# Causal attention in a chained kernel: k's rotation goes ahead a step, and the stage's first steps are put in another order

## What is computed

```python
resid = hidden_states
h = _rmsnorm(hidden_states, ln1_w)
q = (h @ Wq).reshape(B, S, NH, HD)      # NH = 32, HD = 128
k = (h @ Wk).reshape(B, S, KVH, HD)     # KVH = 4
v = (h @ Wv).reshape(B, S, KVH, HD)
q = _rope(q, pos); k = _rope(k, pos)
k = jnp.repeat(k, 8, axis=2); v = jnp.repeat(v, 8, axis=2)
scores = jnp.einsum('bqhd,bkhd->bhqk', q, k) / jnp.sqrt(jnp.float32(HD))
attn = jax.nn.softmax(jnp.where(causal, scores, -1e9), axis=-1)
o = jnp.einsum('bhqk,bkhd->bqhd', attn, v).reshape(B, S, NH * HD) @ Wo
x = resid + o
```

## Time and profile before

| | |
|---|---|
| median of 3 runs | 1162.79 us (1161.12 to 1169.5) |
| profiled execution | 1166.56 us, span 1164.8 us |
| mean granted TensorE clock | 0.955 |
| PE | 1042.5 us busy, 89% of the span |
| PE's weight loads | 914.2 us, 78% |
| DVE | 809.1 us, 69% |
| ACT | 693.8 us, 60% |
| POOL | 639.1 us, 55% |
| causal attention | about 393 to 861 us of the span |

### The profile page before, as it was taken

The page is one execution under the profiler, slowest core; times in us unless marked ns, Lnnn a source line. Parts: engine busy times, 40 slices in busy tenths (PEclk is TensorE's granted clock), DMA queues, the critical chain, the costliest instruction groups (busy, mean ns, idle before and its releaser), DMA issues. The chain is left out here.

```text
span 1164.8 us, 22450 instructions
## 1 busy us (share of the span) xinstructions
PE 1042.5 (89%) x6931; PEld 914.2 (78%) x6931; DVE 809.1 (69%) x1860; ACT 693.8 (60%) x1963; POOL 639.1 (55%) x688
## 2 busy tenths in 40 slices
PE   3798987895999679998999899999979999999998
PEld 3577876784555379888998899899968888888887
DVE  6666675627888868887788788888875555555555
ACT  3455643325899568787887788777843334333342
POOL 5234312441778557775767587666633555555553
PEclk9889989897899779999999999999988999999999
DMA  8000000002213020110011000000011111111111
GB/s 250 1 1 1 2 18 16 1 1 75 89 77 133 13 82 2 47 38 4 2 47 38 4 1 2 2 1 1 2 30 42 41 54 41 54 41 46 49 41 50
DMA packets 44100, 41.78 MB, mean 36 GB/s; under 512 B 6160, under 2 KB 40048, under 8 KB 44000
## 3 DMA queue, kind: packets, MB, share of 16 engines
q1 hardware_dynamic: 42384, 39.54, 11.0%
q10 hardware_dynamic: 1616, 0.99, 0.3%
HBM read 39.40 MB, written 1.11 MB: 35 GB/s over the span
## 5 line engine op out<-in xcount | busy, mean ns | idle before, releaser
L1804 POOL TENSOR_TENSOR prob<-prob,rden 128x128 f32<-128x128 f32 (+1 forms) x256 | 124.8, 509 | 80.4 <-DVE rden L1878 80.3
L2163 POOL TENSOR_TENSOR hid_l<-hid,hid_h 128x512 fp32r<-128x512 f32 x66 | 85.6, 1297 | 134.2 <-ACT hid_h L2132 134.2
L2190 DVE TENSOR_TENSOR hid<-psum,silu 128x512 f32<-128x512 f32 x66 | 45.6, 692 | 125.5 <-ACT silu L2130 125.5
L2130 ACT ACTIVATE silu<-psum 128x512 f32<-128x512 f32 x66 | 39.4, 598 | 117.2 <-PE psum L75 117.2
L2182 DVE SCALAR_TENSOR_TENSOR x<-psum,weight,x 128x256 f32<-128x256 f32 x264 | 108.9, 475 | 0.0
L1753 ACT ACTIVATE prob<-psum,neg_max 128x128 f32<-128x128 f32 (+1 forms) x256 | 105.1, 421 | 5.3 <-issue 3.1
L73 PE MATMUL psum<-xt_h,gu_l 128*128 128x512 f32 x264 | 106.7, 404 | 0.3 <-DVE xt_l L161 0.3
L75 PE MATMUL psum<-xt_h,gu_h 128*128 128x512 f32 x264 | 105.2, 398 | 0.0
L74 PE MATMUL psum<-xt_l,gu_h 128*128 128x512 f32 x264 | 104.8, 397 | 0.0
L1294 POOL TENSOR_TENSOR drive<-u,b_all 128x1024 f32<-128x1024 f32 x32 | 75.4, 2359 | 42.5 <-DVE h L1410 20.7
L1787 POOL TENSOR_TENSOR qr<-r_part_a,r_part_b 128x512 f32<-128x512 f32 x64 | 82.9, 1295 | 8.5 <-DVE r_part_b L1838 8.5
(11 more groups left out here) (281 smaller groups left out, 3728.7 us busy)
## 6 DMA issues: line engine op xcount, KB each, us to landing
b_all<-scan_b_rows SPq DMA_DIRECT2D x16, 512.0 KB, 3.8
early<-in_L_ffn_Wq_dram SPq DMA_DIRECT2D x4, 1024.0 KB, 5.5
early<-in_L_ffn_Wo_dram SPq DMA_DIRECT2D x4, 1024.0 KB, 5.8
raw<-in_L_ffn_Wg_dram SPq DMA_DIRECT2D x32, 128.0 KB, 2.2
raw<-in_L_ffn_Wu_dram SPq DMA_DIRECT2D x32, 128.0 KB, 2.3
raw<-in_L_ffn_Wd_dram SPq DMA_DIRECT2D x32, 128.0 KB, 2.3
x<-_attn_hidden_states_dram SPq DMA_DIRECT2D x8, 128.0 KB, 4.5
early<-in_L_ffn_w_up_q_dram SPq DMA_DIRECT2D x1, 1024.0 KB, 7.1
```

What stands on the lines that cost most here:

```text
L1804: ins = pool.tensor_tensor(at, at, rden[:, s % 4, i:i + 1].to_broadcast([P, (i + 1) * P]), ALU.mult)
L2163: pool.tensor_tensor(hid_l[:, j, cols], hid[:, c, :], f(hid_h[:, j, cols]), ALU.subtract)\
```

## The change

In every batch but the first, DVE's `rotate_k` (v's low part, k's two products) is named in step r = 3, behind `values` and `project_out`, and no longer in r = 4. POOL's sum of the products has a name of its own, `sum_k`, and stands in r = 4 ahead of `split_q`. `turn_k` stays in r = 5.

`FIRST` is laid out anew: q's first pair is projected ahead of k and v, and rotated ahead of k; the second half's normalisation leaves DVE's opening for the piece `normalise_rest` near the end of the list. What was in `norm_rest` (transposes, copies and low parts of half 1, eight z tiles) and the four output-weight pieces of POOL go between the first four steps by the new table `BETWEEN`, z two tiles at a time.

In `Norm`, `stats` is split into `moments` and `variance`; the aggregates now wait for all four statistics of the half. Where the norm is taken twice, the powers are made in the order half 0 first, half 0 second, half 1 first, half 1 second, and DVE's opening follows that. PE's wait for half 1 is added at the first values.

The diff, cut: left out are a line in `normalise` like the one in `again`, and three lists of names handed to `run`.

```diff
@@ -88,9 +88,9 @@
         self.var_ready, self.rstd_ready, self.normed, self.turned, self.hi_ready, self.lo_ready = core.norm_sems
-        rounds = 2 if twice is None else 4
+        self.rounds = (0, 1) if twice is None else (0, 2, 1, 3)
         self.vars_before, self.norms_before = core.norm_vars, core.norms
-        core.norm_vars, core.norms = core.norm_vars + rounds, core.norms + 1
+        core.norm_vars, core.norms = core.norm_vars + len(self.rounds), core.norms + 1
@@ -106,13 +106,19 @@
 
-        own, ts = self.count, slice(h * TH, (h + 1) * TH)
...
             dve.wait_ge(*arrived[h])
+        self.moments(dve, x, h)
+        self.variance(dve, h)
+
+    def moments(self, dve, x, h):
         for t in range(h * TH, (h + 1) * TH):
-            own.add(dve.bn_stats(self.st[:, t, :], x[:, t, :]))
+            self.count.add(dve.bn_stats(self.st[:, t, :], x[:, t, :]))
+
+    def variance(self, dve, h):
+        own, ts = self.count, slice(h * TH, (h + 1) * TH)
+        own.settle()
         for t in range(h * TH, (h + 1) * TH):
-            dve.wait_ge(self.own, own.n - TH + 1)
@@ -126,7 +132,7 @@
         own, ts = self.count, slice(h * TH, (h + 1) * TH)
-        dve.wait_ge(self.rstd_ready, self.vars_before + h + 1)
+        dve.wait_ge(self.rstd_ready, self.vars_before + self.rounds.index(h) + 1)
@@ -185,10 +191,10 @@
     def gpsimd(self, pool, rounds=None):
-        for n in rounds or range(2 if self.twice is None else 4):
+        for n in rounds or self.rounds:
...
             to, src = ((self.rs, self.ve), (self.rs2, self.ve2))[n // 2]
-            pool.wait_ge(self.var_ready, self.vars_before + n + 1)
+            pool.wait_ge(self.var_ready, self.vars_before + self.rounds.index(n) + 1)
@@ -1636,6 +1642,8 @@
                         units[phase] = to, 2 * batch + j // 2, j % 2
+                if more and r == 4:
+                    yield "sum_k", *ahead_b(gg, b + 1)
@@ -1645,14 +1653,14 @@
                     yield "copy_v", *ahead_b(gg, b + 1)
-                if more and r == 4:
-                    yield "rotate_k", *ahead_b(gg, b + 1)
...
                     yield "project_out", *at(-4)
+                if more and r == 3:
+                    yield "rotate_k", *ahead_b(gg, b + 1)
@@ -1661,11 +1669,13 @@
 
-        FIRST = [("kv", 0, 0, 0), ("kv", 0, 0, 1), ("q", 0, 0, 0, 0), ("q", 0, 0, 0, 1), ("copy_v", 0, 0), ("rotate_k", 0, 0),
-                 ("rotate", 0, 0, 0, 0), ("rotate", 0, 0, 0, 1), ("add", 0, 0, 0), ("q", 0, 0, 1, 0), ("q", 0, 0, 1, 1),
-                 ("turn_k", 0, 0), ("split_q", 0, 0, 0), ("norm_rest",), ("scores", 0, 0), ("peak", 0, 0),
-                 ("rotate", 0, 0, 1, 0), ("rotate", 0, 0, 1, 1), ("add", 0, 0, 1), ("q", 0, 1, 0, 0), ("q", 0, 1, 0, 1),
-                 ("rotate", 0, 1, 0, 0), ("q", 0, 1, 1, 0)]
+        FIRST = [("q", 0, 0, 0, 0), ("q", 0, 0, 0, 1), ("kv", 0, 0, 0), ("kv", 0, 0, 1), ("rotate", 0, 0, 0, 0),
+                 ("rotate", 0, 0, 0, 1), ("copy_v", 0, 0), ("rotate_k", 0, 0), ("add", 0, 0, 0), ("sum_k", 0, 0),
+                 ("q", 0, 0, 1, 0), ("q", 0, 0, 1, 1), ("turn_k", 0, 0), ("split_q", 0, 0, 0), ("scores", 0, 0),
+                 ("rotate", 0, 0, 1, 0), ("rotate", 0, 0, 1, 1), ("peak", 0, 0), ("add", 0, 0, 1), ("q", 0, 1, 0, 0),
+                 ("q", 0, 1, 0, 1), ("normalise_rest",), ("rotate", 0, 1, 0, 0), ("q", 0, 1, 1, 0)]
+        BETWEEN = {0: [("z", 0), ("wo_low", 0), ("turn_rest",), ("wo_low", 1)], 1: [("z", 2), ("low_rest",), ("wo_low", 2)],
+                   2: [("z", 4), ("wo_low", 3)], 3: [("z", 6)]}
@@ -1675,7 +1685,10 @@
 
-            all_of([*FIRST, *schedule(0, 0, 4, False)])
+            all_of(FIRST)
+            for n in range(4):
+                all_of(schedule(0, n, n + 1, False))
+                all_of(BETWEEN[n])
@@ -1713,10 +1726,12 @@
 
-                def norm_rest():
+                def turn_rest():
                     norm.scalar(act, (1,))
+
+                def residual(first):
                     act.wait_ge(shifted, 1)
-                    for t in range(NT):
+                    for t in (first, first + 1):
@@ -1779,8 +1794,11 @@
                 pool.wait_ge(norm.normed, NT * norm.norms_before + TH)
-                for piece in Q + O:
+                for piece in Q:
                     weights(0, *piece)
+
+                def wo_low(n):
+                    weights(0, *O[n])
@@ -1793,7 +1811,7 @@
 
-                def rotate_k(g, b):
+                def sum_k(g, b):
@@ -1804,26 +1822,30 @@
 
-                run(pool, dict(add=add, split_q=split_q, rotate_k=rotate_k, softmax=softmax, weights=weights))
+                run(pool, dict(add=add, split_q=split_q, sum_k=sum_k, wo_low=wo_low, softmax=softmax, weights=weights))
...
                 norm.begin(dve)
-                for h in range(2):
-                    norm.stats(dve, core.x, h)
-                for h in range(2):
-                    norm.again(dve, h)
-                dve.scalar_tensor_tensor(shift[:], norm.mv[:, :, 0], -1.0, norm.rs[:], ALU.mult, ALU.mult).then_inc(shifted, 1)
+                norm.moments(dve, core.x, 0)
+                norm.variance(dve, 0)
+                norm.moments(dve, core.x, 1)
+                norm.again(dve, 0)
+                norm.variance(dve, 1)
                 norm.normalise(dve, core.x, 0)
+                norm.again(dve, 1)
...
                                   ALU.mult).then_inc(tables_own, 1)
+                dve.scalar_tensor_tensor(shift[:], norm.mv[:, :, 0], -1.0, norm.rs[:], ALU.mult, ALU.mult).then_inc(shifted, 1)
...
                 norm.low(dve, 0)
-                norm.normalise(dve, core.x, 1)
...
 
-                def norm_rest():
+                def normalise_rest():
+                    norm.normalise(dve, core.x, 1)
+
+                def low_rest():
@@ -1972,6 +1994,8 @@
                     b = s // REP1
+                    if s == 0 and known(g, 1):
+                        norm.ready(pe, 1)
@@ -1995,11 +2019,11 @@
 
-                def norm_rest():
+                def turn_rest():
...
                 run(pe, dict(q=q, kv=kv, turn_k=turn_k, scores=scores, turn_probs=turn_probs,
-                             values=values, project_out=project_out, norm_rest=norm_rest))
+                             values=values, project_out=project_out, turn_rest=turn_rest))
```

More of the change, by code:

```diff
@@ L139, in normalise @@
         if self.twice is not None:
-            dve.wait_ge(self.rstd_ready, self.vars_before + 2 + h + 1)
+            dve.wait_ge(self.rstd_ready, self.vars_before + self.rounds.index(2 + h) + 1)
             own.add(dve.tensor_tensor(self.rs2[:, ts], self.rs2[:, ts], self.rs[:, ts], ALU.mult))
@@ L1766, in _ @@
                 run(act, dict(rotate=rotate, split_q=split_q, turn_k=turn_k, copy_v=copy_v, softmax=softmax, turn_probs=turn_probs, values=values,
-                              weights=weights, norm_rest=norm_rest))
+                              weights=weights, turn_rest=turn_rest, z=residual))
             @block.gpsimd
@@ L1896, in _ @@
                 run(dve, dict(rotate=rotate, rotate_k=rotate_k, turn_k=turn_k, peak=peak, turn_probs=turn_probs,
-                              softmax=softmax, values=values, project_out=project_out, norm_rest=norm_rest))
+                              softmax=softmax, values=values, project_out=project_out, normalise_rest=normalise_rest, low_rest=low_rest))
             @block.tensor
```

## The result

The kernel with the change took 1183.07 us (median of six executions, 1179.32 to 1193.05), the kernel before 1166.61 beside it: a ratio of 1.014, 95% interval 1.0096 to 1.0184. It is slower, by 1.4%. I had forecast no change (1165.4) with a range that ended at 1173.

A forecast was written before the change was run, and what follows sets the result against it. PE was taken to bound causal attention, waiting for k once per batch. Loop +3.6, start -1.5 and norms +0.5 gave +2.6 us on the profiled 1166.56, or 1165.4 against the median 1162.79; range 1153 to 1173.

The forecast's parts named there:

- The bound and the direction of the move: Attention loop: PE sets the pace; its k wait goes and moves one instruction forward, to q's low part, growing a little.
- The loop's price per ordinary batch: Ordinary batch: 1.49 us lost at head 6's scores, 1.16 won at the k transposes, +0.33 in all.
- So that piece has 0.12 us to spare: q's low part ahead of head 6's scores: distance 0.25 us in the ordinary batch against 0.13 where PE waits.
- Step (c): POOL, r = 4: k's sum first (0.69 us), so q's low part ends 1.61 later and head 6's scores start 1.49 later.
- I count nothing for POOL: SBUF port: POOL's pieces kept their length beside DVE's normalisation, so no growth was priced for them.
- rival (C): Step r = 4: DVE's rope product takes the ports ahead of q's low part; 9.8 us more, 1175.2; chance 0.10.
- The sign that I had set for (C): In the profile after, q's low part growing from 0.74 to over 1.2 us would show rival (C).
- The late-weight batches: Three batches with a POOL weight piece ending r = 3: 1.18 us lost against 1.16 or a little more won: 0.
- At the loop's jump: Two batches with the hardware loop's jump between r = 3 and r = 4: k products push it back, +0.3 us each.
- Start: Start of the attention stage, up to the first k transposes in the loop code: -1.5 us in sum.
- my other terms: Start: PE's hole removed -4.11 us, ACT's z and copies given back +2.8, k products holding the reciprocal +0.4.
- Norms: All stages: aggregates waiting for the last statistic cost some 0.1 us per half, +0.5 us in all (0 to 0.8).

The follow-up runs named there:

- pe_kept_busy: Changed kernel plus 16 unread PE transposes of the identity ahead of the wait for q's low part at each head 6: 1176.18 us, ratio 1.0049.
- start_edits_only: Changed kernel with k's products and sum back in their old places in step r = 4, so new start and norm only: 1170.18 us, ratio 1.0039.
- norm_wait_alone: Kernel before with one edit, the aggregates of all norms waiting for the half's four statistics: 1167.11 us, ratio 0.9995.
- k_sum_behind_q_low: Changed kernel with POOL's k sum put behind q's low part in step r = 4: 1160.49 us, ratio 0.9968.
- pe_busy_and_dve_waits: Changed kernel with both PE's 16 added transposes and DVE's wait for q's low part ahead of its sine product: 1178.12 us, ratio 1.0078.
- k_behind_reciprocal_old_start: Kernel before, old start and norm, with k's products right behind the reciprocal and k's sum behind q's low part in r = 4: 1159.26 us, ratio 0.9889.
- loop_edits_only: Kernel before with only k's products in step r = 3 and k's sum ahead of q's low part: 1190.08 us, ratio 1.0191.
- dve_waits_for_q_low: Changed kernel with a wait added: DVE's sine product of step r = 4 starts only when q's low part is done: 1174.42 us, ratio 1.0066.

## Why the prediction was wrong

**The bound and the direction of the move: right.** PE sets the pace, the k wait went, and in all 15 batches PE waits for q's low part at the scores of head 6. The k side brought what I said: 4.37 to 3.23 is 1.14 us (I had 1.16).

**The loop's price per ordinary batch: the failed step.** I had 1.49 us lost at the scores of head 6. It was 5.28 - 3.24 = 2.04, and 3.6 where the clock fell. Two terms stood at nothing, POOL's own pieces growing beside DVE and PE's clock falling in the longer wait; in the 15 batches they cost some 6.8 (0.45 each) and 9.3 us. Three things make up the difference:

1. *"So that piece has 0.12 us to spare"*: it had none. With DVE's move alone the scores came 0.90 later, with POOL's order alone 0.67; both blocks are paid almost in full. Step (c) said 0.92 + 0.69 = 1.61 less the 0.12 = 1.49, and it is 0.90 + 0.67 = 1.57. I had taken the 0.12 from two kinds of batch, 0.25 behind q's low part against 0.13. But in the kernel after the ordinary batch waits 2.20 us for that piece and still starts 726.63 - 726.39 = 0.24 behind it: the longer distance was no slack.
2. *"I count nothing for POOL"*, in the part on the port. q's low part grew from 0.74 to 1.17 in all 15 batches. This was rival (C), with the right place and point of decision; I had priced it at 0.7 a batch, and it is 0.45. The row I argued from, POOL's pieces beside DVE's normalisation, was another case: it scales one tile and is no product of two, and DVE was the one that came second (its first piece started at 404.77, POOL's at 404.67, and so on through all four). The sign that I had set for (C), over 1.2, was a little high. Taking the collision away brought the 0.45 back, so it is shown. In the batch shown, DVE's product begins beside the k sum, and ends at 725.81, 0.59 into q's low part, which ends at 725.22 + 1.17 = 726.39. The Trainium skill, SBUF — State Buffer, section Summary: rules for kernel authors, says that the second of such a pair waits until the first is done; by that q's low part would have ended at 725.81 + 0.73 = 726.54, so the trace agrees, to 0.15 us. The rule held for POOL as well as for DVE, and I had weighed it by DVE's rows alone.
3. *The clock, in no step of the sum.* A wait of 1.1 us had left it at 1.00 in all 15 batches of the profiled kernel before. In the kernel after it fell in 6 of 15, about 1.55 us each: 9.3 of the 17.9 us. Four of these stand behind the twelve holes of 2.07 us and more, two at the loop's jumps, where PE stands still twice, the second time for 1.44 and 1.19 us. With the loop edits alone it was 7 of twelve such holes and one jump. It is shown by pe_kept_busy, where the wait stays and the fall goes. The Trainium skill, TensorE: Matmul & The Clock Gate, section HAM oscillation — how this bites in real kernels, warns that gaps in PE's work let the clock drop, by the example of a kernel whose gaps are longer than these. The trace agrees that gaps do it, and shows it behind holes of 2.10 to 2.22 us. Why it falls behind some of these equal holes and not behind others stays open; in two kernels (start_edits_only and norm_wait_alone) it fell once at a hole of 1.03 and 1.04 us, with one of 0.69 just ahead of it, and in four (k_sum_behind_q_low, pe_kept_busy, pe_busy_and_dve_waits, k_behind_reciprocal_old_start) once at a jump of the loop.

Beside these, in the third batch of a group, step r = 6 took 3.75 instead of 3.03 because POOL's weight piece was late behind the hole and q's low part behind that: +0.7 in two batches. The late-weight batches were right at about nothing (8.40 against 8.26 us for r = 4 and 5 in the one of the three where the clock stayed). At the loop's jump I had +0.3 each: +0.5 and +0.3, before the fall that each of the two had.

**Start: the sum right, in part by luck.** -1.5 forecast, -1.34 measured (head 8's scores at 50.65 us of the stage instead of 51.99). The first matmul comes 1.0 earlier instead of 0.6, and what is won behind it is 0.3 instead of the 0.9 that my other terms give, so two misses nearly cancel. The second normalisation takes 1.38 us instead of 5.25, and the 4.11 us hole is gone. The rows of after that answer to the earlier trace rows:

```profile
400.65 0.58 PE L73 MATMUL psum<-xt_h,wq_l 128*128 128x256 f32 x1 [3.04 <-POOL wq_l L1792]
...
413.88 1.38 DVE L155 TENSOR_SCALAR norm_y<-x,ln_mean_var,ln_rstd 128x256 f32<-128x256 f32 x4
```

**Norms: right in kind.** 0.1 us a half, too small to be seen in the total; the statistics' rows of after:

```profile
390.07 1.40 DVE L116 BATCH_NORM_STATS2 ln_stats<-x 128x6 f32<-128x256 f32 x4 [0.55 <-PEq L1277]
391.51 0.38 DVE L122 BATCH_NORM_AGGREGATE ln_mean_var<-ln_stats 128x2 f32<-128x6 f32 x4
```

**The range.** Its upper end, 1173, lies under the 1175.2 that I had worked out for (C) itself, and it had nothing for the clock. With the collision (6.8 us) and the falls (9.3) my +2.6 becomes +18.7, and the stage shows +17.9.

## What to carry to other kernels

Where each engine works its pieces in one order, a piece moved forward pushes all that stands between, so look first at which of those PE needs next: here the two moves cost 0.90 and 0.67 us at one wait to save 1.14 at another, while the same products right behind the reciprocal, and the sum left behind q's low part, kept most of the gain (0.81 of the 1.14 us a batch; -13.0 us of stage instead of +17.9). Before making one wait longer by joining it with others, ask for the clock: holes of 2 us in PE's work were followed by a fall 11 times in 24 here, at 1.5 us each. And when blocks shift, lay the shifted times of DVE's products on two SBUF operands over POOL's pieces, since the collision moves too.

## What was not expected of the hardware

- POOL's piece of 0.73 us takes 1.17 to 1.19 when DVE's product of 128x512 on two SBUF operands gets in ahead of it, and DVE's takes 1.05 instead of 0.7 when it comes in behind a POOL piece, and 1.70 beside a weight piece of 1.29. Which of two POOL pieces pays is decided by which stands second (q's low part in the kernel after, the k sum in k_sum_behind_q_low).
- The granted clock was 0.64 over 4.8 us behind a hole of 2.2 us and back at 1.00 after that. Between batches with the same hole it fell in some only: behind holes of 2.06 to 2.24 us in 4 of 12 (the kernel after) and 7 of 12 (loop_edits_only), behind holes of 1.61 to 1.76 us in 2 of 12 (dve_waits_for_q_low).
- Sixteen transposes that nobody reads, in a hole of 2.2 us, made the stage 9.0 us shorter. At the loop's jump, where PE was late anyway, they cost 0.6 (5.53 against 4.95).
